# Token norm, attention and mixture-of-experts layer: x's transposes taken by token tile, the second feature half rounded by VectorE beside ScalarE, two warming products fewer

## The reference

```
xn   = layernorm(x)                                   # over the 256 features
q, k = elu(xn @ Wq) + 1, elu(xn @ Wk) + 1 ; v = xn @ Wv
att  = q * scan(k * v) / clip(sum(q * scan(k)), 1e-6) # scan: s = sigmoid(decay) * s + input, per head, 16 heads
attn = att @ w_out
e    = argmax(xn @ router_w.T) ; gate = sigmoid(max logit)      # one of 8 experts
moe  = expert_e(gate * xn) + shared_expert(xn)        # each: silu(g) * u, then down
out  = x + attn + moe
```

## Time and profile before

| | |
|---|---|
| median of 3 executions | 129.44 us (129.26 to 131.13) |
| the profiled execution | 129.56 us |
| its span, first to last instruction | 127.9 us |
| PE busy | 122.5 us (96% of the span) |
| VectorE busy | 79.7 us (62%) |
| ScalarE busy | 52.4 us (41%) |
| GpSimd busy | 35.2 us (28%) |
| transfers | 25.02 MB, mean 196 GB/s |

### The profile page before, as it was taken

The page is one execution under the profiler, slowest core; times in us unless marked ns, Lnnn a source line. Parts: engine busy times, 40 slices in busy tenths (PEclk is TensorE's granted clock), DMA queues, the critical chain, the costliest instruction groups (busy, mean ns, idle before and its releaser), DMA issues.

```text
span 127.9 us, 2432 instructions
## 1 busy us (share of the span) xinstructions
PE 122.5 (96%) x826; PEld 106.6 (83%) x826; DVE 79.7 (62%) x176; ACT 52.4 (41%) x111; POOL 35.2 (28%) x63
## 2 busy tenths in 40 slices
PE   4989999999999999999999999999999999999990
PEld 1258767787888667999999999999999978999990
DVE  0899886999999977755575553515140428922371
ACT  1665796979954725422222222242121337200000
POOL 6804000007888200030303030303030301687500
PEclk9999999999999999999999999999999999999999
DMA  3681999999992210129888988889782031033427
GB/s 95 204 275 60 308 356 243 173 255 399 394 350 109 82 51 0 46 60 293 286 284 290 272 318 264 319 255 336 255 310 75 1 94 51 17 92 96 117 97 243
DMA packets 15748, 25.02 MB, mean 196 GB/s; under 512 B 1296, under 2 KB 12632, under 8 KB 15736
## 3 DMA queue, kind: packets, MB, share of 16 engines
q1 hardware_dynamic: 13368, 20.66, 51.2%
q0 software_dynamic: 1456, 3.41, 8.0%
q10 hardware_dynamic: 912, 0.80, 1.9%
HBM read 18.78 MB, written 6.08 MB: 194 GB/s over the span
## 4 chain that ended last, share of the span: by engine, by line
PE 80%; POOL 6%; issue 5%; DMA 4%; DVE 2%; ACT 0%; DVEq 0%; POOLq 0%
PE ps L1105 25%; PE ps L1119 13%; POOL q_sb L450 6%; PE ps L295 5%; PE ps L296 5%; PE ps L297 5%; PE ps L965 5%; PE ps L971 4%; PE ps L978 4%; PE ps L1049 4%; DMA q_sb<-sorted_rows,slot_row 2%; PE ps L1036 2%; DMA sorted_rows<-yrow 2%; PE ps L1043 2%; DVE x_sb L889 1%
## 5 line engine op out<-in xcount | busy, mean ns | idle before, releaser
L1105 PE MATMUL ps<-xgT,gu 128*128 128x144 f32 x256 | 34.0, 286 | 0.0
L1105 PEld LDWEIGHTS ps<-xgT,gu 128*128 128x128 f32 x256 | 32.3, 190 | 0.3 <-ACT xgT L528 0.2
L820 DVE TENSOR_TENSOR wqkv<-rz,ps 128x288 f32<-128x288 f32 x16 | 7.3, 454 | 25.9 <-ACT rz L564 25.8
L432 POOL DMA_DIRECT2D sorted_rows<-yrow x9 | 5.0, 560 | 55.5 <-DVE yrow L815 55.5
L1119 PE MATMUL ps<-wqkv,dn 128*128 128x144 f32 x128 | 17.4, 289 | 0.0
L564 ACT ACTIVATE rz<-ps 128x288 f32<-128x288 f32 x16 | 6.6, 411 | 25.4 <-PE ps L1105 25.4
L424 POOL DMA_INDIRECT sorted_rows<-xn,slot_row x8 | 11.2, 1396 | 19.0 <-ACT xn L500 17.2
L1119 PEld LDWEIGHTS ps<-wqkv,dn 128*128 128x128 f32 x128 | 16.1, 190 | 0.0
L295 PE MATMUL ps<-xT_hi,sgu_hi 128*128 128x512 f32 x32 | 13.0, 405 | 0.0
L296 PE MATMUL ps<-xT_lo,sgu_hi 128*128 128x512 f32 x32 | 12.5, 390 | 0.0
L297 PE MATMUL ps<-xT_hi,sgu_lo 128*128 128x512 f32 x32 | 12.5, 390 | 0.0
(11 more groups left out here) (162 smaller groups left out, 230.3 us busy)
## 6 DMA issues: line engine op xcount, KB each, us to landing
gu<-in_L_ffn_w_gate_up_dram SPq DMA_DIRECT2D x8, 1024.0 KB
dn<-in_L_ffn_w_down_dram SPq DMA_DIRECT2D x8, 512.0 KB
sorted_rows<-zeros SPq DMA_DIRECT2D x1, 2592.0 KB, 17.8
wqkv<-sorted_rows SPq DMA_DIRECT2D x10, 144.0 KB
sorted_rows<-yrow POOLq DMA_DIRECT2D x9, 128.0 KB, 2.1
sgu<-_ffn_shared_gate_up_dram SPq DMA_DIRECT2D x1, 1024.0 KB, 6.1
wqkv<-in_L_attn_w_qkv_dram SPq DMA_DIRECT2D x3, 256.0 KB, 3.7
x_sb<-in_L_attn_x_dram SPq DMA_DIRECT2D x2, 256.0 KB, 3.7
```

The lines of the kernel that those rows point to most:

```text
L820: V.tensor_tensor(hr[:, 2 * h:2 * h + 2, :].rearrange("p f s -> p (f s)"), act_sb[:, h, 0:2 * SLOTS], ps[:, 2 * h + 1, 0:2 * SLOTS], ALU.m ...
L1105: ins = mm(ps[:, 2 * h + u, (f % 2) * SLOTS:(f % 2 + 1) * SLOTS], gu[p][:, kc, col:col + P], xgT[:, kc, :], start=(kc == 0), stop=(kc == K ...
```

## The change

Four things are edited. `WARM` goes from 14 to 12. `transpose_tokens` goes over the token tiles outside and over the two feature halves inside, for both token halves, and each half's semaphore increment is at token tile `j == 2`, the last one. For the first token half, ScalarE rounds feature half 0 alone, and VectorE rounds feature half 1 (a copy out of PSUM with its own semaphore `s_xhi_dve`). On VectorE, `x_lo(0)` stands directly behind that copy, and the statistics of token tiles 4 and 5 come behind it. The thresholds of `s_xhi` follow.

```diff
-WARM = 14
+WARM = 12
@@ ScalarE, x_hi
-                for c in range(KC):
+                for c in range(n + 1):
@@ VectorE, x_lo
-                    dve.wait_ge(s_xhi, 2 * n + c + 1)
+                    if n == 0 and c == 1:
+                        dve.wait_ge(s_xhi_dve, 1)
+                    else:
+                        dve.wait_ge(s_xhi, n + c + 1)
@@ VectorE, the start
             w_lo(1).then_inc(s_wlk, 1)
+            dve.wait_ge(s_xT, KC)
+            V.tensor_copy(xT_hi[:, 1, 0:512], ps[:, 5, :]).then_inc(s_xhi_dve, 1)
+            x_lo(0)
             for i in range(TH, TH + 2):
                 statistics(i)
-            x_lo(0)
@@ TensorE, transpose_tokens
-                for c in range(KC):
-                    for j in (0, 3, 1, 2):
-                        if c == 0:
-                            if j == 3:
-                                pe.wait_ge(s_xna, n + 1)
-                            else:
-                                pe.wait_ge(s_xn, 3 * n + j + 1)
+                for j in (0, 3, 1, 2):
+                    if j == 3:
+                        pe.wait_ge(s_xna, n + 1)
+                    else:
+                        pe.wait_ge(s_xn, 3 * n + j + 1)
+                    for c in range(KC):
                         ins = tr(ps[:, 4 + c, j * P:(j + 1) * P], xn[:, n * TH + j, c * P:(c + 1) * P], ident[:, :])
-                    ins.then_inc(s_xT, 1)
+                        if j == 2:
+                            ins.then_inc(s_xT, 1)
@@ TensorE, router_logits
-                pe.wait_ge(s_xhi, 2 * n + 2)
+                pe.wait_ge(s_xhi, 2 * n + 1)
@@ TensorE, qkv_tile, hi_hi
-                            pe.wait_ge(s_xhi, kc + 1)
+                            pe.wait_ge((s_xhi, s_xhi_dve)[kc], 1)
```

More of the change, by code:

```diff
@@ L202, in build @@
         s_xhi = sem("s_xhi")
+        s_xhi_dve = sem("s_xhi_dve")
         s_xlo = sem("s_xlo")
```

## The result

Over 22 executions the changed kernel has a median of 130.91 us (130.12 to 132.56), the kernel before 129.52 us (129.26 to 131.47). The ratio is 1.0081, with a 95% interval of 1.0054 to 1.0109 (executions over 1.5% above the fastest of their kernel, five of the changed one's, are left out of it, and it is not the ratio of the medians). The forecast was 130.0 us in a range of 129.2 to 131.2. The sign and the range held. The loss is larger than the 0.47 us summed up: 0.92 between the two profiled executions, 1.39 between the medians. The fastest executions of the two differ by 0.86 us, and the changed kernel's fall into groups, which a median hides: eleven at 130.12 to 130.48, six at 131.33 to 131.68, five at 132.17 to 132.56. The median lies in the gap between the first two, where no execution is.

A forecast was written before the change was run, and what follows sets the result against it. PE, full from 18.2 us on, was taken to bound the kernel through tile 4's first product. Terms of -0.13, +0.18, +0.25 and +0.17 summed to 0.47 us late: 130.0 us, range 129.2 to 131.2.

The forecast's parts named there:

- The sum: All terms added: everything from 18.2 us on 0.47 us late, 130.0 us, with lower and upper ends 129.6 and 130.4.
- What bounds the kernel: PE is busy throughout from 18.2 to 104 us, so the start of tile 4's first product decides the time.
- Warming products, at no cost: At the start on PE: two fewer products cost nothing and free PE for the transposes 0.79 us sooner.
- rival B: TensorE's clock rises late because fewer warming products leave pauses on PE; 1.87 us more, 131.9 us, chance 0.14.
- Term 1: VectorE's copy for feature half 1, 0.61 us to the next start: tile 0's last product 0.13 us sooner.
- The prediction's first place: Low half of xT: VectorE ends at 10.20, PE's product starts at 10.45, read as 0.25 us from end to product.
- Term 2: Statistics behind x_lo(0) delay VectorE's v weights' low part to 10.74 and tile 1's product with it: +0.18 us.
- The q weights' low part on GpSimd ends at 12.29 and is not moved: GpSimd's subtraction for the q weights keeps its 10.99 start and 1.30 us length despite VectorE's later work.
- Term 3: VectorE 0.54 us late delays xn of token tile 7, so the second half's transposes wait on PE: +0.25 us.
- Term 4: Token order in the second half: feature half 0 completes later, ScalarE's roundings start 0.62 us later; +0.17 us more.
- The two branches: The logits' products and k's combination both lead to tile 4's first product, forecast to meet there at 18.69.
- Nothing behind 18.2 us is edited: From tile 4's first product to 104 us all work shifts by the same amount, with no further loss.

The follow-up runs named there:

- e1: The kernel before with 12 warming products in place of 14, nothing else; 129.54 us against 129.89, ratio 0.9973.
- e7: The changed kernel with the second token half's transposes back in feature order; 131.47 us, ratio 1.0112 to the kernel before.
- e6: The changed kernel without the split: ScalarE rounds both halves, VectorE has no copy; 130.13 us against 129.72 for the kernel before.
- e4: The changed kernel with the v weights' low part made by GpSimd instead of VectorE; 129.95 us against 129.89 for the kernel before.
- e2: The kernel before with the transposes by token tile in both halves, nothing else; 130.39 us against 129.89, ratio 1.0029.
- e3: The changed kernel with 14 warming products and the old order of the transposes; 132.01 us, ratio 1.016 to the kernel before.
- e5: The changed kernel with GpSimd's q weights' low part held until VectorE finished the v weights' one; 130.92 us, ratio 1.0102 to the kernel before.
- e9: The changed kernel run again, unaltered; 130.99 us, ratio 1.0085 to the kernel before.
- e10: The changed kernel with token tile 6's statistics ahead of VectorE's v weights' low part, so GpSimd's subtraction starts first; 131.49 us, ratio 1.0145 to the kernel before.
- e11: As e10, with GpSimd's subtraction also waiting for VectorE's; 131.30 us, ratio 1.0123 to the kernel before.

## Why the prediction was right, and where its sum fell short

- **The range**: held in part by luck. The sum's own band was 129.6 to 130.5, and the median of 130.91 is outside it. Half of the executions are at 131.33 and more; one more of them, and the median would have been over 131.2.
- **What bounds the kernel**: right. PE is full from tile 4 on, and what happens before 18.2 us is carried to the end, with one exception of 0.15 us.
- **Warming products, at no cost**: right for the kernel before (e1), where all twelve were long and no time was lost; rival B's 131.9, at 0.14, is not what a late clock costs. But the 0.79 us by which PE would be free sooner hang on the clock: it was 0.96 in the change's first profile (7.40 to 6.44) and 0.41 in e7 (to 6.99), where the copy then waited.
- **Term 1, the copy**: its length was taken from the subtraction, 0.61 to the next start; it was 0.61 (8.36 to 8.97), and the second xT_lo was at its place to 0.01 us once x's landing is taken off. e6 shows that it delayed VectorE's next work by only 0.07 us; its further price, at 24 us and in the race, was not in the sum. The prediction's first place, the product at 10.45, was misread: PE's products are 0.23 to 0.24 us apart there before (10.21, 10.45, 10.68), so PE set the 10.45 itself, and the 0.25 us from VectorE's end to a product is no release. In the changed kernel, where PE did wait, it is 0.06 (10.25 to 10.31 and 11.58 to 11.64). The sum got away with it, since token tile 7 comes later and decides.
- **Term 2, the statistics behind x_lo(0)**: right in size on VectorE (10.73 against 10.74), too large on PE: tile 1's product came at 11.64, against 11.84 with x's 0.17 in. "The q weights' low part on GpSimd ends at 12.29 and is not moved" was the wrong step. It ended at 12.72, and the pairing matters: before, VectorE's subtraction was through at 10.88 and GpSimd's started at 10.99. The change puts VectorE's start at 10.7 to 10.9, on top of GpSimd's. If VectorE is first, GpSimd alone waits, and there is slack; if GpSimd is first, VectorE loses 1.0 us, and tile 4 starts 0.8 to 1.2 us later than in the change (19.80, 19.86 and 20.16 against 18.96). The forecast had neither case; the first costs nothing, so only the second was missed in the time.
- **Term 3, token tile 7**: right; PE waited 0.37 us, 0.43 was summed. e4 shows that this path is the one that counts.
- **Term 4, token order**: right in size (ScalarE's rounding at 15.85, against 15.84 with x's 0.17 in). The two branches did not meet: tile 4 waited for k's combination alone, and that last step was short by 0.09. e2 shows the size of the order without the rest, 0.66 us over both halves. In the change the first half's share is paid back by the two products.
- **"Nothing behind 18.2 us is edited", so nothing is lost there**: wrong by 0.15 us. VectorE's backlog of 1.0 us met a slack of 0.19 in the shared expert's low weights. I had read that PE was never idle there before, but not by how little.
- **The sum**: 0.47 forecast. In the profiled execution 0.92: 0.47 as forecast, 0.17 the landing of x, 0.15 the shared expert, 0.09 the step from k's combination to tile 4; the remaining few hundredths I can't place. Over all executions comes the lost race.

What stays open: the gap of 0.5 us on VectorE at 24 us, which is in every profile with the copy and VectorE's own v low part (the change, e3, e5, e7, e9, e10, e11), in which VectorE has one instruction more than before, and in none of the others; and whether the executions of the change at 131.3 to 131.7 are all lost races, since only profiled executions show the two lengths. e3, e7 and e10, at 131.87, 131.33 and 131.20 with VectorE at 1.64 to 1.68, make it likely; what sets the order of the two in an execution is the landing of x and of the q weights and, by e7, the clock, and no experiment took these apart.

## What to carry to other kernels

Work moved on one engine has to be laid beside the other engines' instructions at its new time, not only beside what waits for it: two instructions that never met can meet, and here the price of a lost meeting (1.0 us) was twice the sum of everything counted. Where a queue becomes late, look for the next places with little slack on it all the way down, and write down each slack, because "not waited for" and "0.19 us early" read the same in a table of busy time. And where executions fall into groups, profile more than one: the first profile here was of the lucky group.

## What the runs showed of the hardware

- A VectorE subtraction with both inputs in SBUF and a GpSimd subtraction did not run side by side. The second to start took 1.64, 1.67 and 1.68 us in place of 0.68 on VectorE (e7, e3, e10), and 1.55, 1.74, 1.79 and 1.82 in place of 1.30 on GpSimd (e2, e6, e9, the change). VectorE's ended 0.55 us after GpSimd's, GpSimd's 1.14 to 1.15 us after VectorE's, in each of them.
- VectorE subtractions with one input in PSUM kept their 0.68 us beside GpSimd's (e4: VectorE 9.82 to 10.50, GpSimd 9.71 to 11.00).
- The clock column of the busy-time view reads 1.00 from the first microsecond, while the warming products are 0.58 to 0.63 us long for as much as their whole series (e1, e7) and 0.39 later: the lengths show the two levels, 1.2 and 2.4 GHz, and that column does not there.
- The last indirect gather landed after 2.79 us in one execution and 4.59 in another of the same program (the change, e9).
